# One norm's input transposed by the host: mean rows subtracted from it, the inverse deviation applied to gates and normaliser, token centres on ScalarE

## What is computed

```python
def _layernorm(x, axis=-1, eps=1e-05):
    m = jnp.mean(x, axis=axis, keepdims=True); v = jnp.var(x, axis=axis, keepdims=True)
    return (x - m) / jnp.sqrt(v + eps)
# attention, for each of 8 heads of 64 features; q from the normed x, k = v = context
ig, fg = concat(q, k, v) @ igate_kernel + igate_bias, concat(q, k, v) @ fgate_kernel + fgate_bias
cs = cumsum(log_sigmoid(fg))                       # over the tokens
log_D = where(lower triangle, cs - cs.T, -inf) + ig.T
max_log_D = max(log_D, -1);  D = exp(log_D - max_log_D)
C = (q @ k.T / sqrt(64)) * D
normalizer = maximum(abs(C.sum(-1)), exp(-max_log_D))
h = C / (normalizer + 1e-6) @ v;  h = h * rsqrt(mean(h*h) + 1e-6)
x = x + tanh(g_xattn) * h
# feed-forward, act_quant to 8 bits a row, weight_quant to -1, 0, 1 times one scale
g, u = act_quant(layernorm(x)) @ weight_quant(w_gate).T, act_quant(layernorm(x)) @ weight_quant(w_up).T
x = x + tanh(g_ffn) * (act_quant(relu(g)**2 * u) @ weight_quant(w_down).T)
```

## Time and profile before

| | us |
|---|---|
| three runs | 600.03, 599.99, 600.42; median 600.03 |
| the profiled execution | 600.03, of which the span on the core is 598.3 |
| PE busy | 565.5 (95%) |
| DVE busy | 525.9 (88%) |
| ACT busy | 452.9 (76%) |
| POOL busy | 129.4 (22%) |
| chain that ended last | PE 79%, ACT 8%, DVE 6% |
| granted PE clock, mean | 0.994 |

### The profile page before, as it was taken

One profiled execution on the slowest core, in us unless ns is written; L12 is line 12 of the kernel. 1 busy time (PEld: TensorE's weight loads), 2 busy tenths in 40 slices (PEclk: granted clock), 3 DMA queues, 4 the chain that ended last, 5 costly groups with the idle time before them and its releaser, 6 DMA issues.

```text
span 598.3 us, 18337 instructions
## 1 busy us (share of the span) xinstructions
PE 565.5 (95%) x6506; PEld 339.5 (57%) x6587; DVE 525.9 (88%) x1151; ACT 452.9 (76%) x926; POOL 129.4 (22%) x284
## 2 busy tenths in 40 slices
PE   8986679999999999999999999999999999999997
PEld 4744435656565655656565665656565565656454
DVE  4799898989989898998989898998989899897965
ACT  4799889686876869687786868687786868777563
POOL 3267142130301212120221213020121212021100
PEclk9999989999999999999999999999999999999999
DMA  8968050050605023050503205050502305030001
GB/s 302 383 237 300 23 175 22 28 187 3 213 0 194 18 84 127 18 193 0 199 13 140 72 31 181 0 211 0 194 18 89 122 18 194 3 107 2 19 36 36
DMA packets 44257, 62.68 MB, mean 105 GB/s; under 512 B 1864, under 2 KB 25920, under 8 KB 44224
## 3 DMA queue, kind: packets, MB, share of 16 engines
q1 hardware_dynamic: 44224, 62.24, 29.5%
HBM read 53.72 MB, written 8.51 MB: 104 GB/s over the span
## 4 chain that ended last, share of the span: by engine, by line
PE 79%; ACT 8%; DVE 6%; issue 5%; POOL 1%; DMA 1%; SPq 0%; DVEq 0%; ACTq 0%; POOLq 0%
PE gb L1226 16%; PE ub L1226 16%; PE yb L1252 16%; PE tp L1273 8%; PE ab L1260 7%; PE ab L1240 4%; PE tp L1300 3%; PE ab L1283 3%; PE ab L1261 2%; ACT wdT L531 1%; ACT wgT L539 1%; POOL stage L449 1%; PE ab L1334 1%; ACT relu L549 1%; DVE stage L816 1%
## 5 line engine op out<-in xcount | busy, mean ns | idle before, releaser
L1226 PE MATMUL gb<-wgT,xqT 128*128 128x512 bf16 x486 | 126.9, 381 | 4.0 <-issue 3.9
L1226 PE MATMUL ub<-wuT,xqT 128*128 128x512 bf16 x492 | 127.2, 380 | 1.6 <-DVE stage L816 0.3
L1252 PE MATMUL yb<-wdT,stage 128*128 128x512 bf16 x466 | 112.0, 383 | 6.7 <-ACT stage L561 3.4
L547 ACT ACTIVATE relu<-gb 128x512 f32<-128x512 f32 x128 | 75.2, 587 | 46.0 <-PE gb L1226 45.6
L816 DVE TENSOR_TENSOR stage<-relu,ub 128x512 f32<-128x512 f32 x128 | 86.8, 678 | 15.7 <-ACT relu L549 15.5
L1226 PEld LDWEIGHTS ub<-wuT,xqT 128*128 128x128 bf16 x512 | 49.2, 98 | 62.6 <-DVE stage L816 4.7
L549 ACT ACTIVATE relu<-relu 128x512 f32<-128x512 f32 x128 | 80.7, 631 | 4.1
L943 DVE SCALAR_TENSOR_TENSOR dmat<-ab,dmat 128x384 f32<-128x384 f32 x128 | 65.1, 549 | 18.7 <-POOL dmat L457 13.0
L1252 PEld LDWEIGHTS yb<-wdT,stage 128*128 128x128 bf16 x496 | 45.9, 98 | 50.7 <-ACT stage L561 3.5
L1226 PEld LDWEIGHTS gb<-wgT,xqT 128*128 128x128 bf16 x512 | 45.9, 100 | 45.0 <-issue 1.0
L457 POOL TENSOR_SCALAR_AFFINE_SELECT dmat<-dmat 128x256 f32<-128x256 f32 x128 | 55.5, 461 | 58.8 <-ACT dmat L607 46.7
(11 more groups left out here) (139 smaller groups left out, 899.5 us busy)
## 6 DMA issues: line engine op xcount, KB each, us to landing
dmat<-max_rows SPq DMA_DIRECT2D x15, 1024.0 KB, 5.0
values<-in_ctx_v SPq DMA_DIRECT2D x16, 520.0 KB, 7.6
xs<-in_x SPq DMA_DIRECT2D x16, 512.0 KB, 5.8
cT<-in_ctx_t SPq DMA_DIRECT2D x16, 512.0 KB, 6.8
out<-stage SPq DMA_DIRECT2D x31, 256.0 KB, 2.0
stage<-in_w_gate SPq DMA_DIRECT2D x4, 1024.0 KB, 13.0
stage<-in_w_up SPq DMA_DIRECT2D x4, 1024.0 KB, 13.4
stage<-in_w_down SPq DMA_DIRECT2D x4, 1024.0 KB, 6.6
```

What stands on the lines that cost most here:

```text
L547: nc.scalar.activation(relu[:, c % 2, :], gb[c % 2][:, :], ACT.Relu).then_inc(g_free, 1)
L1226: last = nc.tensor.matmul(bank[c % 2][:, :], xqT[par][:, t, d, :], w[:, d, c * CH:(c + 1) * CH], start=(d == 0), stop=(d == KD - 1))
L1252: done = nc.tensor.matmul(yb[:, :], hqT[:, c, :], wdT[:, c, :], start=(c == 0), stop=(c == KF - 1))
```

## The change

The host adds an input `x_t`, x transposed to features by tokens. For sequences 2 to 15 SP loads it straight into `qT`, right behind the load of x (512 KB a step), and `attention_norm`, `q_columns` and `columns` are gone. In their place:

- PE's `mean_rows(b,m)`, two transposes of the means spread over 128 columns, into bank `yb`; it stands behind `chunk(b,0,2)`, in front of scores 4.
- DVE's `centre_queries(m)`, two 128x512 subtractions of these rows from `qT`, in place; it stands behind `hidden(b,0,1)`, in front of `weigh` 4. `down(b-1,1)` waits for it, since it writes `yb`.
- The gates of context and of queries are accumulated apart; `gates_in` becomes two multiplications by `rstd` and an addition.
- ACT makes the deviation `std` with one more small Exp; POOL multiplies the normaliser's floor by it in two small instructions, and the 1e-6 becomes 1e-6 times `std`.

Three further edits: the second half of `hidden_cols(b-1,1)` (bank `ab[1]`) goes from DVE to ACT, in front of `heads(n,3)`; the subtraction of `token_centres` goes from DVE (L1010) to ACT from sequence 2 on, with the sign turned, behind `hidden_cols(b,0)`, which moves in front of `tokens_rstd`, while DVE does `hidden(b,1,1)` ahead of the maxima; and one `keep_warm(6)` of the prologue becomes `keep_warm(19)`.

```diff
@@ SP
             def load(n, par):
                 for t in range(T):
                     sp.wait_ge(x2_ready[t], n - 1)
                 queries(n, par)
+                turned(n, par)
                 keys(n, par)
                 padded_values(n, par)
@@ POOL
+            def normaliser_floor(n, npar):
+
+                gp.wait_ge(std_ready, n - 1)
+                gp.wait_ge(enm_ready, n + 1)
+                alone(gp, gp_passed)
+                spread = std[npar][:, :, None].to_broadcast([P, T, NH])
+                nc.gpsimd.tensor_tensor(enm[npar][:, :, :], enm[npar][:, :, :], spread, ALU.mult).then_inc(floor_ready, 1)
+                nc.gpsimd.tensor_scalar(floor_eps[:, :], std[npar][:, :], NORM_EPS, 0.0, ALU.mult, ALU.add).then_inc(floor_ready, 1)
...
                     masks(n, 3)
+                    if not at(n, 0, 1):
+                        normaliser_floor(n, 1 - par)
@@ ACT
+                if not at(m, 0, 1):
+                    nc.scalar.activation(std[par][:, :], lnv[:, :], ACT.Exp, scale=0.5).then_inc(std_ready, 1)
+
+            def token_centres(n, npar):
+
+                act.wait_ge(ln2_step, LN2_K * n + 4)
+                for t in range(T):
+                    nc.scalar.activation(xm[:, t, :], x2[npar][:, t, :], ACT.Identity, scale=-1.0,
+                                         bias=mv2[:, t, 0:1]).then_inc(centred, 1)
...
                 if prev and n is not None:
                     hidden_cols(b - 1, 1)
+                    hidden_cols(b - 1, 1, 1)
                 if n is not None:
                     heads(n, 3)
                     squares(n)
-                if m is not None:
-                    for t in range(T):
-                        columns(m, qT[par], t)
                 quantise_high(b, 0)
...
-                if m is None:
-                    hidden_cols(b, 0)
-                if n is not None:
+                hidden_cols(b, 0)
+                if n is not None:
+                    if not third:
+                        token_centres(n, npar)
                     tokens_rstd(n)
-                if m is not None:
-                    hidden_cols(b, 0)
@@ DVE
+            def centre_queries(m, par):
+
+                dve.wait_ge(rows_full, m - 1)
+                dve.wait_ge(xt_in[par], turned_loads(m, par))
+                for t in range(T):
+                    half = qT[par][:, :, t * P:(t + 1) * P]
+                    mean_row = yb[:, None, t * P:(t + 1) * P].to_broadcast([P, KD, P])
+                    nc.vector.tensor_tensor(half, half, mean_row, ALU.subtract).then_inc(q_ready, 1)
...
+                    dve.wait_ge(rstd_step, RSTD_K * (m + 1))
+                    for t in range(T):
+                        nc.vector.scalar_tensor_tensor(gates[:, t, :], of_queries[:, t, :], rstd[:, t:t + 1], gbias[:, t, :],
+                                                       ALU.mult, ALU.add).then_inc(gate_scaled, 1)
+                    dve.wait_ge(gate_scaled, T * (m - 1))
+                    nc.vector.tensor_tensor(gates[:, :, :], gates[:, :, :], of_context, ALU.add).then_inc(tp_free, 1)
...
                 hidden(b, 0, 1)
+                if m is not None:
+                    centre_queries(m, par)
                 if n is not None:
                     weigh(n, 4)
                     weigh(n, 5)
...
-                if m is not None:
-                    attention_norm(m, par)
                 hidden_max(b, 0, 0)
                 if not prev:
                     magnitudes(2, 3)
                 hidden(b, 0, 3)
-                if prev and n is not None:
-                    hidden_cols(b - 1, 1)
                 hidden_max(b, 0, 1)
...
-                if n is not None:
-                    token_centres(n, npar)
+                if prev:
+                    hidden(b, 1, 1)
+                if n is not None:
+                    token_maxima(n, npar)
                 if not prev:
                     scale_weight(2, 3)
-                else:
-                    hidden(b, 1, 1)
@@ PE
+            def mean_rows(b, m):
+
+                pe.wait_ge(stat_step, STAT_K * (m + 1))
+                if at(b, 0):
+                    pe.wait_ge(winv_step, WSUM[1])
+                else:
+                    pe.wait_ge(o_ready, 2 * b - 1)
+                alone(pe, pe_passed)
+                for t in range(T):
+                    last = nc.tensor.transpose(yb[:, t * P:(t + 1) * P], mv[:, t, 0:1].to_broadcast([P, P]), ident[:, :])
+                last.then_inc(rows_full, 1)
...
             max_columns(1)
-            keep_warm(6, ub[1])
+            keep_warm(19, ub[1])
             weight_total(1)
...
                 chunk(b, 0, 2, par)
+                if m is not None:
+                    mean_rows(b, m)
                 if n is not None:
                     scores(n, 4, npar)
                     scores(n, 5, npar)
...
-                if m is not None:
-                    q_columns(m, par)
                 if prev:
-                    down(b - 1, 1, 0, KF // 2)
+                    down(b - 1, 1, 0, KF // 2, m)
@@ host
+    laid["x_t"] = laid["x"].transpose(0, 2, 1)
```

More of the change, by code:

```diff
@@ L23 @@
 STAT_K, RSTD_K, Q_K = 4, 2, 2
[L24 removed]
+GATE_K, POST_K, LN2_K = 3, 11, 11
 QUANT_K = 6
@@ L30, with gated_block @@
 GATE_TILES = 4
-def gated_block(nc, x, ctx_t, ctx_v, small_in, w_gate, w_up, w_down, max_rows, out):
+def gated_block(nc, x, x_t, ctx_t, ctx_v, small_in, w_gate, w_up, w_down, max_rows, out):
     B, S, D = x.shape
@@ L93, in gated_block @@
         rstd = sb("rstd", [P, T], F32)
+        std = [sb(f"std{i}", [P, T], F32) for i in range(2)]
+        floor_eps = sb("floor_eps", [P, T], F32)
         q = sb("q", [P, T, D], F32)
@@ L176, in gated_block @@
         x_in = [sem(f"x_in{i}") for i in range(2)]
+        xt_in = [sem(f"xt_in{i}") for i in range(2)]
         ct_in = [sem(f"ct_in{i}") for i in range(2)]
@@ L182, in gated_block @@
         q_ready = sem("q_ready")
+        rows_full = sem("rows_full")
+        std_ready = sem("std_ready")
+        gate_scaled = sem("gate_scaled")
+        floor_ready = sem("floor_ready")
+        centred = sem("centred")
+        centred_here = sem("centred_here")
         tp_full = sem("tp_full")
@@ L238, in bank_order @@
                     uses.append(("hidden", b - 1, 1))
-                if m is not None:
-                    uses.append(("column", m, 0))
                 uses.append(("hidden", b, 0))
@@ L955, in normaliser @@
                 dve.wait_ge(post_step, k + 1)
-                nc.vector.tensor_scalar(nrm[:, :, :], nrm[:, :, :], NORM_EPS, None, ALU.add).then_inc(post_step, 1)
+                if at(n, 0, 1):
+                    nc.vector.tensor_scalar(nrm[:, :, :], nrm[:, :, :], NORM_EPS, None, ALU.add).then_inc(post_step, 1)
+                else:
+                    nc.vector.tensor_tensor(nrm[:, :, :], nrm[:, :, :], floor_eps[:, :, None].to_broadcast([P, T, NH]),
+                                            ALU.add).then_inc(post_step, 1)
                 dve.wait_ge(post_step, k + 2)
@@ L1241, in hidden_transposes, with down @@
                     last.then_inc(a_full[e], 1)
-            def down(b, t, first, last):
+            def down(b, t, first, last, m=None):
                 for c in range(first, last):
@@ L1247, in down @@
                         pe.wait_ge(o_ready, 2 * b + t)
+                    if c == 0 and m is not None:
+                        pe.wait_ge(q_ready, Q_K * (m + 1))
                     if c % (KF // 2) == 0:
@@ L1294, in gate_products @@
                             pe.wait_ge(ct_in[par], loads_of(m, par))
+                        elif at(m, 0, 1):
+                            pe.wait_ge(a_free[t], column_use(m) + 1)
                         else:
-                            pe.wait_ge(a_free[t], column_use(m) + 1)
+                            pe.wait_ge(q_ready, Q_K * m + t + 1)
                     src, row = (cT[par], KD + kd) if part == 0 else (qT[par], kd)
                     width = P // tiles
+                    whole = at(m, 0, 1)
+                    col = t if whole else T * part + t
                     for g in range(tiles):
-                        done = nc.tensor.matmul(tp[width * g:width * (g + 1), t * 2 * NH:(t + 1) * 2 * NH],
+                        done = nc.tensor.matmul(tp[width * g:width * (g + 1), col * 2 * NH:(col + 1) * 2 * NH],
                                                 src[:, kd, t * P + width * g:t * P + width * (g + 1)], gk[:, row, :],
-                                                start=(part == 0 and kd == 0), stop=(part == 1 and kd == KD - 1))
+                                                start=(kd == 0 and not (whole and part == 1)),
+                                                stop=(kd == KD - 1 and not (whole and part == 0)))
                         if j == T * 2 * KD - 1:
@@ L1475, in _ @@
                 done.then_inc(y_full, 1)
-_INS = ["x", "ctx_t", "ctx_v", "small", "w_gate", "w_up", "w_down"]
```

(1 more changed line is left out.)

70 lines of the change are left out of this document (41 added, 29 removed).

## The result

The changed kernel takes 616.31 us (median of 4 runs, 616.11 to 616.73), the kernel before 600.02 us beside it (599.99 to 600.42): recorded ratio 1.0265, 95% interval 1.0252 to 1.0277 (the two medians divided give 1.0271). It is slower, as forecast; 613.8 us was 2.5 us too low. The span of the profiled execution grew from 598.3 to 614.6 us, by 16.3.

A forecast was written before the change was run, and what follows sets the result against it. PE and DVE were both taken to be on the edge, with hidden(b,1,0) setting the step. 600.03 us + 12.0 (13 steps of 0.92) + 1.8 (prologue) + 0 (steps 14 and 15) = 613.8 us, range 600 to 618.

The forecast's parts named there:

- The bound: PE and DVE both on the edge in the step's first part; any delay of hidden(b,1,0) is a longer step.
- the second of the three places: PE's cumulative_sum waits for the gates' logf, with a reserve of about 0.4 us.
- Steps 1 to 3: PE's mean_rows 0.27 us, DVE's centring pair 1.21; weigh 4 and what follows on PE 0.64 us later.
- the sign I gave, 2.6: Scores 6 would start 2.6 us after the end of chunk(b,0,2), not 1.7.
- Steps 4 and 5: ACT's ab[1] eviction makes heads(n,3) end at 9.17, not 8.03; DVE's normaliser waits, starting at 9.24, not 8.63.
- Step 6: DVE's gates_in, three instructions in place of one: +0.30 us, bounds 0.2 and 0.5; nabs 0.92 late.
- Step 7: DVE's chain from nabs to hidden(b,1,0) keeps its length, 6.31; PE's bank at 20.19, not 19.27: +0.92 us a step.
- What was costed at nothing: Token centres on ACT (up to 1.3 us without cover), small Exp, POOL's two instructions, and the 512 KB load.
- The prologue: 13 more warm matmuls start weight_scale(1) 1.9 us later, step 0 gives part back: +1.8 us, bounds 0 and 2.8.
- The end: Steps 14 and 15: heads(n,3) late but PE not held by gates; 0 us, bounds -0.5 and +0.5.
- Faster: PE sets the step, 0.95 us shorter: 589.5 us; any gain needs heads(n,3) to end before 8.25; chance 0.13.
- Half of it: Centring costs only the transposes' 0.27 us in place of 0.64: step +0.5, 608.7 us; chance 0.18.

The follow-up runs named there:

- f3_three_pad_early: Changed kernel with 13 warm matmuls in step 0, ab[1] eviction behind squares(n), centring behind weigh 7, hidden(b,1,0) ahead of token_stats (steps 1 to 13): 604.60 us.
- e1: Also e1_cols_behind: changed kernel with ACT's eviction of ab[1] moved behind heads(n,3) and squares(n): 607.43 us, ratio 1.0110 to the kernel before.
- e3_warm6: Changed kernel with keep_warm(6) again in place of keep_warm(19) ahead of weight_total(1): 655.91 us, ratio 1.0907 to the kernel before.
- f1_pad_step0: Changed kernel with the 13 added warm matmuls moved from the prologue into step 0, ahead of scores 6: 611.76 us, ratio 1.0188 to the kernel before.
- both links shortened: Changed kernel with 13 warm matmuls in step 0, ab[1] eviction behind squares(n) on ACT and centring behind weigh 7 on DVE: 606.12 us.
- the best order tried: Changed kernel, matmuls in step 0, ab[1] eviction and centring later; on DVE hidden(b,1,0), gates, logf and cumulative(m) earlier (steps 1 to 13): 603.38 us.

## Why the prediction was right, and where not

- **The bound.** Right. "Any delay of `hidden(b,1,0)` is a longer step" held in the changed kernel; the second part of the step stayed at 14.79. But it isn't the only edge: with `hidden(b,1,0)` moved ahead (`f3_three_pad_early`) the step falls by 0.2 only, and `cumulative_sum` holds it, the second of the three places that I had named.
- **Steps 1 to 3.** DVE starts centring at 0.42 (forecast 0.48), the pair takes 1.28 and `weigh` 4 starts at 1.63 (forecast 1.69), `chunk(b,0,3)` at 3.54 (forecast 3.62). Scores 6 start at 2.23 by their row, in place of 1.71 by a row of the same shape; `mean_rows` takes 0.32, not 0.27; the sign I gave, 2.6, contradicts my own steps, since 0.64 behind 1.71 is 2.35. The bounds of the centring, 0.91 and 1.4, held, and the middle form was right.
- **Steps 4 and 5.** Right to 0.1 us, the wait and its releaser included, and e1 shows it by taking it away. ACT's new pair is 1.94 long, as 1.014 with the overlap of 0.1 gives.
- **Step 6.** Mis-sized. From the first gate instruction to nabs is 0.61 us where it was 0.22: +0.39, not +0.30, inside the bounds of 0.2 and 0.5. The Trainium skill's rule ("VectorE: DVE Perf Modes", The DRAIN you can't avoid), by which the gates add 0.2, is further off. The error of the steps ahead, -0.1, hid this: nabs is late by exactly the forecast 0.92.
- **Step 7.** From nabs to `hidden(b,1,0)` DVE takes 6.43 and 6.26 us in turn, where 6.31 was forecast, so the first part is 20.29 and 20.12. Together with the second part (-0.1) the steps are 0.92 and 0.75 longer, 0.82 to 0.84 on average. Thirteen steps gave 10.99 us, not 12.0. That odd and even steps differ by 0.17 I had not looked for.
- **What was costed at nothing.** The token centres took 1.32 for the pair and ended at 21.15 (forecast 21.1); the small steps behind DVE's maxima began at 22.06 (forecast 21.8), and PE reached `token_columns` 1.03 later than before without a wait. The load of the transposed x landed in 7.0 us. Both free, as said.
- **The prologue.** The step that failed: 1.8 us were forecast, with bounds of 0 and 2.8, and 4.37 + 0.61 = 4.98 measured. The direct delay was as forecast (2.0 behind the start of the stretch, against 1.9). What failed is "Step 0 gives back part of it (no `q_columns`, no copies)". It gives nothing back and costs 2.2 us of its own, as `e3_warm6` shows without the thirteen matmuls (44.85 against 42.62). I counted what step 0 loses and put what it gains at nothing, though the steps 1 to 6 of my own sum, the centring ahead of `weigh` 4, the late heads and the longer gates, hold in step 0 as well: 0.9 us to `logf`, and 1.3 more at the lower clock behind PE's wait for it. The remaining 0.6, ahead of the stretch, is within what the same code differs by. The end, costed at 0, took 0.33. By terms: 613.8 - 1.0 (steps) + 3.2 + 0.3 is the 616.3 measured. So the 2.5 us by which the total missed are smaller than the 3.2 by which the prologue did: the steps' error, of the other sign, hid a part, and that was luck. And the thirteen matmuls were no pure cost: they hold the loop where its body isn't fetched anew. No view of the kernel before could have said so, nor did I ask for the packets.
- **The rivals.** "Faster" fell by the sign it was given: the whole chain would have had to bring `heads(n,3)` to an end by 8.25, and it ended at 9.10. With both links shortened it ends at 8.34, just outside, and the kernel is still slower than before, as is the best order tried (603.38). "Half of it" didn't happen, as the pair took the forecast form (its sum was off, too: thirteen steps of +0.5 are 6.5 us, not 6.9, so 608.3). The result lies 1.7 us under the range's upper end: with the prologue's true bounds that end would have been some 620.

## What to carry to other kernels

Work taken from the busiest engine is worth its time only if the next engine's deliveries move with it. Here PE was relieved of 1.22 us a step, less 0.32 for the new transposes, while DVE's work fell by 0.35 (4.2 us over twelve steps) and its deliveries came later: count the date of each delivery, not busy times. An eviction moved onto an engine with idle time costs what stands behind it, and much more once the cover on the waiting engine is gone (0.13 us a step alone, 0.48 with the rest of the change). Follow a change through the steps that are written out as well as through the loop: step 0 had the loop's loss, too. Warm-up matmuls that seem to be padding may also set where the loop starts in the instruction stream: after any edit ahead of a large loop compare the packets of the instruction queue.

## What the runs showed of the hardware

- Thirteen matmuls fewer ahead of the loop, and nothing else changed: 655.91 us in place of 616.31, 65 instruction packets in place of 20, PE standing about 4 and up to 2 us for its own instructions at the start of each of five turns. The kernel before has the smaller number there and 20 packets.
- PE's idle 2.85 us in step 0 was followed by eight matmuls of 128x512 that took 3.48 us at a granted clock of 0.51. With thirteen matmuls in the place of this wait the same eight took 1.83, at full clock (`f1_pad_step0`).
- The same wait of 2.76 us, with the same code ahead of and behind it, was followed by a granted clock of 0.58 over 4 us in one execution (the changed kernel) and by full clock in another (`e1_cols_behind`): 6.81 and 5.49 us for the same work.
- In the changed kernel odd and even steps differ by 0.17 us, in what DVE takes from nabs to `hidden(b,1,0)` (6.43 and 6.26). Its cause wasn't looked for.
